# Rotary attention in a decoder kernel: another order of the steps around the softmax, and the keys' addition on another engine

## The reference

```python
def _L1_attn_ref(x, W_qkv, W_o1, W_o2, gamma):      # called with _layernorm(x), its result is added to x
    qkv = x @ W_qkv
    q, k, v = jnp.split(qkv, 3, axis=-1)
    q, k, v = (to_heads(q), to_heads(k), to_heads(v))
    apply_rope = lambda t: t * cos + rotate_half(t) * sin
    q, k = (apply_rope(q), apply_rope(k))
    dots = jnp.einsum('bhid,bhjd->bhij', q, k) * scale
    dots = jnp.where(causal, neg, dots)
    attn = jax.nn.softmax(dots, axis=-1)
    out = jnp.einsum('bhij,bhjd->bhid', attn, v)
    out = out.transpose(0, 2, 1, 3).reshape(b, n, INNER)
    out = jax.nn.relu(out @ W_o1) @ W_o2
    mean = jnp.mean(out, axis=-1, keepdims=True)
    var = jnp.var(out, axis=-1, keepdims=True)
    ...
```

## Time and profile before

| | before |
|---|---|
| median of 3 runs | 1791.98 us (1784.16 to 1795.23) |
| the profiled execution | 1798.92 us, span 1797.1 us |
| TensorE busy, share of the span | 1206.6 us, 67% |
| VectorE | 1063.3 us, 59% |
| ScalarE | 626.0 us, 35% |
| GpSimd | 665.7 us, 37% |
| first and last start of the stage (first transpose L1707 to the next stage's first, L550) | 385.1 and 636.7 us |

### The profile page before, as it was taken

How to read it: one execution, slowest core, us unless ns; L and a number is a source line. 1 busy time by engine, 2 the same in 40 slices (tenths; PEclk the granted TensorE clock), 3 DMA queues, 4 the chain that set the end, 5 groups by cost and what they waited for, 6 DMA issues and landing times. The chain is left out here.

```text
span 1797.1 us, 35666 instructions
## 1 busy us (share of the span) xinstructions
PE 1206.6 (67%) x14040; PEld 918.3 (51%) x14040; DVE 1063.3 (59%) x2911; ACT 626.0 (35%) x1479; POOL 665.7 (37%) x729
## 2 busy tenths in 40 slices
PE   7882438827888679374667444199839857666888
PEld 5652437726766646362345343088715616253556
DVE  4879611156999758615776657234379854444773
ACT  2541113306666646023553111022124334333443
POOL 3337444423555445532223114623343331413320
PEclk9885569969999889585877655599978765656788
DMA  9900046440000094040000010345310000000000
GB/s 256 132 2 2 29 118 179 143 130 2 3 2 3 3 136 58 17 120 3 1 1 16 9 24 7 102 139 179 120 35 2 1 1 2 1 1 1 1 2 24
DMA packets 74059, 90.19 MB, mean 50 GB/s; under 512 B 5823, under 2 KB 61186, under 8 KB 73248
## 3 DMA queue, kind: packets, MB, share of 16 engines
q1 hardware_dynamic: 67872, 77.94, 18.6%
q0 software_dynamic: 6016, 9.93, 1.6%
HBM read 57.60 MB, written 32.69 MB: 50 GB/s over the span
## 5 line engine op out<-in xcount | busy, mean ns | idle before, releaser
L846 POOL TENSOR_TENSOR arena<-arena,small 128x1024 f32<-128x1024 f32 x96 | 184.4, 1926 | 154.4 <-ACT arena L704 90.7
L394 POOL TENSOR_SCALAR var_eps<-moments 128x1 f32<-128x1 f32 (+1 forms) x136 | 33.6, 247 | 405.9 <-DVE moments L387 405.9
L606 PE MATMUL ps<-arena,q 64*64 64x512 f32 x768 | 129.9, 751 | 57.8 <-issue 20.6
L755 ACT ACTIVATE arena<-arena 128x1024 f32<-128x1024 f32 x92 | 97.3, 1058 | 179.1 <-DVE arena L920 127.9
L616 PEld LDWEIGHTS ps<-small,arena 128*128 128x128 f32 x736 | 101.8, 167 | 82.6 <-ACT arena L755 48.0
L616 PE MATMUL ps<-small,arena 128*128 128x128 f32 x736 | 124.0, 323 | 24.3 <-ACT arena L755 22.7
L628 PE MATMUL ps<-vx,arena 128*64 128x18 f32 x3072 | 126.6, 228 | 3.7 <-issue 3.0
L628 PEld LDWEIGHTS ps<-vx,arena 128*64 128x64 f32 x3072 | 116.5, 160 | 24.3 <-issue 20.4
L795 ACT COPY arena<-ps 128x512 f32<-128x512 f32 x192 | 104.6, 586 | 53.3 <-PE ps L616 52.3
L1857 POOL TENSOR_TENSOR arena<-arena 128x512 f32<-128x512 f32 x64 | 79.8, 1282 | 104.2 <-DVE arena L1875 104.2
L396 POOL TENSOR_TENSOR rstd<-var_eps,minus_half 128x1 f32<-128x1 f32 (+1 forms) x136 | 105.3, 774 | 11.3
(11 more groups left out here) (324 smaller groups left out, 2786.0 us busy)
## 6 DMA issues: line engine op xcount, KB each, us to landing
expert_ring<-L2f_in SPq DMA_DIRECT2D x23, 704.0 KB, 4.2
expert_ring<-L0f_in SPq DMA_DIRECT2D x23, 578.0 KB
slots_L0f<-blank SPq DMA_DIRECT2D x1, 8385.0 KB, 56.9
slots_L2f<-blank SPq DMA_DIRECT2D x1, 8385.0 KB, 56.8
small<-small_in SPq DMA_DIRECT2D x1, 4231.5 KB, 19.2
expert_ring<-L1f_in SPq DMA_DIRECT2D x8, 512.0 KB
arena<-slots_L0f SPq DMA_DIRECT2D x23, 129.0 KB, 3.1
arena<-slots_L2f SPq DMA_DIRECT2D x23, 129.0 KB, 3.6
```

The lines of the kernel that those rows point to most:

```text
L606: last = pe.matmul(c.ps[part(b), m], c.q[part(m), at:at + S], kx(t)[part(m), b * 512:(b + 1) * 512], start=True, stop=True)
L755: act.activation(buf(k), buf(k), ACT.Relu if sparse else ACT.Exp, scale=exp_scale).then_inc(s.probs_ready, 1)
L846: g.tensor_tensor(kx(t).rearrange("p (b h k) -> p b h k", b=2, k=S), bcast(of_tile, 2, HEADS // 2), bcast(bcast(c.w("head_of_row"), 2, S), ...
```

## The change

VectorE adds the products of the keys (`add_turned_keys`), GpSimd keeps those of the queries. In VectorE's step the measuring of `att` and the normalising now stand behind the maxima and ahead of the products, and they work on tiles one step older (k-4 and k-2). TensorE's `project_values` moves to the end of the step and works on the next tile; weighing and both output projections work on tile t-3, and the weighing stands ahead of the turning. ScalarE's exponentials are split 10, 2 and 4, with the copies of the weighed values (k-3) in front of those of the turned probabilities. A fourth place for values is the buffer `q`, which this sub-layer did not use. The three instructions of the residual become two `scalar_tensor_tensor`. GpSimd's second inversion works on tile k-4 in place of k-5.

```diff
-    values = lambda t: c.room(4 + t % 3)
+    value_places = [c.room(4), c.room(5), c.room(6), c.q[:]]
+    values = lambda t: value_places[t % 4]
...
-            for t in range(NT + 2):
+            for t in range(NT + 3):
                 if t < NT:
-                    project_values(t)
                     project(t, 0)
                     project(t, 1)
-                if t >= 2:
+                if t == 0:
+                    project_values(0)
+                if t >= 3:
+                    weigh_values(t - 3)
+                if 0 <= t - 2 < NT:
                     turn_probs(t - 2)
-                    weigh_values(t - 2)
-                    project_out(t - 2)
+                if t >= 3:
+                    project_out(t - 3)
                 if t < NT:
                     scores(t)
-                if t >= 2:
-                    project_mid(t - 2)
+                if t >= 3:
+                    project_mid(t - 3)
+                if t + 1 < NT:
+                    project_values(t + 1)
...
+            def take_values(t):
+                act.wait_ge(s.v_ps, t + 1)
+                if t >= 4:
+                    act.wait_ge(s.o_ps, t - 3)
+                act.copy(values(t), c.ps[:, 4:6].rearrange("p b n -> p (b n)")).then_inc(s.v_ready, 1)
...
+            for k in range(NT + 4):
+                if 0 <= k - 4 < NT:
+                    take_mid(k - 4)
+                if k < NT:
+                    take_values(k)
+                if 0 <= k - 1 < NT:
+                    soften(k - 1, range(10))
+                if 0 <= k - 3 < NT:
+                    take_weighed(k - 3)
+                if 0 <= k - 1 < NT:
+                    soften(k - 1, range(10, 12))
+                if 0 <= k - 2 < NT:
+                    take_turned_probs(k - 2)
+                if 0 <= k - 1 < NT:
+                    soften(k - 1, range(12, 16))
+                if 0 <= k - 3 < NT:
+                    rectify(k - 3)
...
                 if k < NT:
-                    for i, signal in enumerate((s.q_rotated, s.k_rotated)):
-                        g.wait_ge(s.by_sin, 2 * k + i + 1)
-                        for half in range(2):
-                            own_half = rotated[i][:, half * 512:(half + 1) * 512]
-                            g.tensor_tensor(own_half, own_half, sines[i][:, (1 - half) * 512:(2 - half) * 512], ALU.add)\
-                                .then_inc(signal, 1)
-                if 0 <= k - 5 < NT:
-                    invert(c, g, following, k - 5)
+                    g.wait_ge(s.by_sin, 2 * k + 1)
+                    for half in range(2):
+                        own_half = rotated[0][:, half * 512:(half + 1) * 512]
+                        g.tensor_tensor(own_half, own_half, sines[0][:, (1 - half) * 512:(2 - half) * 512], ALU.add)\
+                            .then_inc(s.q_rotated, 1)
+                if 0 <= k - 4 < NT:
+                    invert(c, g, following, k - 4)
...
+            def add_turned_keys(t):
+
+                v.wait_ge(s.by_cos, 2 * t + 2)
+                v.wait_ge(s.by_sin, 2 * t + 2)
+                for half in range(2):
+                    own_half = rotated[1][:, half * 512:(half + 1) * 512]
+                    v.tensor_tensor(own_half, own_half, sines[1][:, (1 - half) * 512:(2 - half) * 512], ALU.add)\
+                        .then_inc(s.k_rotated, 1)
...
             for k in range(NT + 6):
-                softened = 0 <= k - 1 < NT
-                if softened:
+                if 0 <= k - 1 < NT:
                     mask(k - 1)
                     find_max(k - 1)
+                if 0 <= k - 4 < NT:
+                    v.wait_ge(s.y_ready, k - 3)
+                    measure(v, own, c.att, k - 4)
+                if 0 <= k - 2 < NT:
+                    normalise(k - 2)
                 if k < NT:
                     rotate(k, 0)
                     rotate(k, 1)
+                    add_turned_keys(k)
                 t = k - 4
                 if 0 <= t < NT:
-                    scale(v, own, c.att, c.hn, t)
-                    v.wait_ge(own.normed, t + 1)
-                    v.tensor_tensor(c.hn[:, t], c.hn[:, t], c.w("L1_gamma"), ALU.mult).then_inc(s.weighted, 1)
+                    v.wait_ge(own.rstd, t + 1)
+                    v.scalar_tensor_tensor(out=c.hn[:, t], in0=c.att[:, t], scalar=own.moments_of[:, t, 0:1],
+                                           in1=c.w("L1_gamma"), op0=ALU.subtract, op1=ALU.mult).then_inc(s.weighted, 1)
                     v.wait_ge(s.weighted, t + 1)
-                    v.tensor_tensor(c.x[:, t], c.x[:, t], c.hn[:, t], ALU.add).then_inc(s.added, 1)
+                    v.scalar_tensor_tensor(out=c.x[:, t], in0=c.hn[:, t], scalar=own.rstd_of[:, t:t + 1],
+                                           in1=c.x[:, t], op0=ALU.mult, op1=ALU.add).then_inc(s.added, 1)
                     v.wait_ge(s.added, t + 1)
                     measure(v, following, c.x, t)
                 if 0 <= k - 5 < NT:
                     scale(v, following, c.x, c.h, k - 5)
-                if 0 <= k - 3 < NT:
-                    v.wait_ge(s.y_ready, k - 2)
-                    measure(v, own, c.att, k - 3)
-                if softened:
-                    normalise(k - 1)
```

More of the change, by code:

```diff
@@ L1689, in rotary_attention @@
     scores_ps = c.ps[:, 0:4, 0:256].rearrange("p r (m k) -> p r m k", k=S)
-    exps_of = lambda t: 2 + 3 * t if t < NT else 0
     head_of = lambda block, u: 8 * (block % 2) + 4 * u + block // 2
@@ L1800, in soften @@
             def soften(t, groups):
+                act.wait_ge(s.bias_ready, t + 1)
                 for g in groups:
@@ L1805, in soften, with take_mid, take_weighed, take_turned_probs @@
                                           accum_out=c.row_max[:, t, g:g + 1])
[L1806 to L1811, removed]
-                if 0 <= k - 3 < NT:
[L1813 to L1828, removed]
+                if groups[-1] == HEADS - 1:
+                    last.then_inc(s.exp_ready, 1)
+            def take_mid(t):
+                act.wait_ge(s.y_ps, t + 1)
+                act.copy(c.att[:, t], c.ps[:, 7, 0:P]).then_inc(s.y_ready, 1)
+            def take_values(t):
[3 more added lines that the diff above has]
+                act.copy(values(t), c.ps[:, 4:6].rearrange("p b n -> p (b n)")).then_inc(s.v_ready, 1)
+            def take_weighed(t):
+                act.wait_ge(s.o_ps, t + 1)
+                if t > 0:
+                    act.wait_ge(s.mid_ps, t)
+                for b in range(2):
+                    act.copy(outT[:, b * 512:(b + 1) * 512], c.ps[:, 6 + b]).then_inc(s.o_ready, 1)
+            def take_turned_probs(t):
                 for j in range(2):
@@ L1833, in _, with rectify @@
                     act.copy(probsT[:, j * 512:(j + 1) * 512], c.ps[:, 4 + j]).then_inc(s.probsT_ready, 1)
[L1834 to L1842, removed]
+            def rectify(t):
                 act.wait_ge(s.mid_ps, t + 1)
                 act.activation(c.oT[:, tok(t)], c.ps[:, 6, 0:P], ACT.Relu).then_inc(s.mid_ready, 1)
+            for q in range(QUARTERS):
+                act.wait_ge(s.turned_ps, q + 1)
+                act.copy(c.hT[:, quarter(q)], c.ps[:, q]).then_inc(s.turned, 1)
+            for k in range(NT + 4):
[15 more added lines that the diff above has]
+                    rectify(k - 3)
         @block.gpsimd
@@ L1894, in normalise @@
                 shaped = by_position(probs(t))
-                v.wait_ge(s.exp_ready, exps_of(t))
+                v.wait_ge(s.exp_ready, t + 1)
                 v.reciprocal(c.row_inv[:, t], c.row_max[:, t]).then_inc(s.inv_ready, 1)
```

## The result

The changed kernel takes 1802.64 us (median of 19 runs, 1792.7 to 1816.1), the kernel before 1793.12 in the same comparison: ratio 1.0068, 95% interval 1.0045 to 1.009. It is slower by 0.7%, and 1768 was forecast. The spans of the profiled executions lie 7.1 us apart (1804.2 after, 1797.1 before). Of these 4.5 are the rotary stage, 256.1 us (378.18 to 634.24) in place of 251.6; the parts ahead of it and behind it, whose instructions are unchanged, differ between the profiled executions of this document by up to 12 us (ahead) and 14 us (behind). The medians lie 9.5 apart; what the stage costs is taken from the traces.

What follows compares the result with a forecast made beforehand. The prediction took VectorE, or the chain through it, to bound the rotary stage. Fill 7.5 plus steady part 17.9 less drain 1.4 gave 24 us, from the median of 1791.98 to 1768, range 1758 to 1781.

Steps and rivals of the forecast that it cites:

- the cover on TensorE: TensorE's work within a step fits under the new pace: queries' half at +5.8 against VectorE's 6.06, covered by 0.3 us.
- the sum's steady part: Rotary tiles 3 to 15: 12 steps of 12.2 us, 146.5 in place of 164.5, summed as a gain of 17.9.
- The clock rival: TensorE's clock falls in the rotary stage's steady part: a step near 19 us, four eat the gain; 3 in 100.
- GpSimd's last 5.01 lie bare on the path: Of 7.69 us from first product to scores, GpSimd's four additions fill the last 5.01 and hold up the scores.
- 1.52 a step: Gain from VectorE adding the keys' products: scores start 6.17 us after the first product instead of 7.69.
- +12.2: TensorE's path through projections, weighing and ScalarE's copies lets the next scores start 12.2 us after the last scores' start.
- off the path: Three-instruction residual's 1.2 us each in the shadow of GpSimd's additions: said not to set the step, counted as nothing.
- its three pieces: Rotary step: scores to mask 1.64 us, mask to first product 4.42, first product to scores 6.17.
- no starving: Rival: VectorE's key additions each meet a GpSimd addition and cost 1.69 us, 2.0 a step more, 1800; 4 in 100.
- The ScalarE loop: Rival: output projection waits for ScalarE's copies; if 0.9 us late, a step is 12.7, total 1774; 12 in 100.
- The fill: Start of the rotary stage up to tile 3's scores: 7.5 us gained, up to 4 more if TensorE's clock stays high.
- The drain: From the last scores to the next stage's first transpose: one more round, 30.3 us instead of 28.9, loss 1.4.

Runs made afterwards that it cites:

- the half-page kernel: Changed kernel with 32 small matmuls (128 TensorE instructions) ahead of the rotary stage and 32 behind it: 1772.41 us, 0.9897 of the kernel before.
- the whole page: Changed kernel with 64 small matmuls (256 TensorE instructions) ahead of the rotary stage and none behind: 1.0047 of the kernel before.
- the kernel before moved: Kernel before with 23 small matmuls ahead of the rotary stage and 41 behind, so its scores fall on one instruction page: 1831.23 us, ratio 1.0219.

## Why the prediction was wrong

**The step that failed** is the cover on TensorE: "values 1.85 behind the scores' start", taken with "the scores, which take 1.59" and "The mask starts at 1.64 behind the scores' start (1.59 and a signal)". These durations hold only as long as TensorE has its instructions, and the sum put the wait for them at nothing. The change takes 164 instructions out of TensorE's stream ahead of tile 3's scores (one weighing, one output projection, one last projection, all now a step later), which puts the scores onto one packet; the kernel before has the same number a step, but its packets end inside the scores' first third and ahead of the turning. Its rotary stage shows no stop, and the prediction never counted instructions. The sign was there in another stage, where the same wait stands at 54 us, with a packet that landed at 52.42:

```profile
50.50 0.93 PE L628 MATMUL ps<-vx,arena 128*64 128x18 f32 x25
54.02 0.50 PE L628 MATMUL ps<-vx,arena 128*64 128x18 f32 x7 [2.58 <-issue]
```

The runs put a number on it: 172.8 us for the twelve steps with stops, 147.3 without, so 25.6 us were lost. The eight stops are 14.8 of that; of the other 10.8, by subtraction, 9.7 stand in the five steps in which TensorE's clock fell behind the stop. With that, the sum's steady part, forecast as a gain of 17.9, became a loss of 8.3.

**The clock rival** named the right engine and the wrong cause. I argued that there would be "no gap as long as the 5.8"; in or right behind a stop of 1.7 to 2.1 inside the scores the granted clock fell in five of eight cases. It carried 3 in 100.

**A reading that was wrong and did no harm.** The prediction says of the 7.69 from first product to scores that "GpSimd's last 5.01 lie bare on the path". Two paths ended together there: GpSimd's additions at 552.35 and TensorE's output projection, behind ScalarE's copies, at 552.66 (550.61 and 2.05), and the scores at 552.59 show no wait. With the keys' additions alone the 7.69 stays. Of a step of 13.80 they take 0.56 in the old order, the new order alone takes 0.14, and both together 1.53, so the "1.52 a step" wasn't a gain "of this part". The sum came out right because the cover counted the second path too, to "+12.2". The residual's waits for GpSimd did not lie "off the path" either: in the run with the keys' additions alone they are gone, and the mask comes 0.93 sooner although VectorE has those additions as well.

**What held**, measured where the stops are absent. The step: 12.27 against 12.2, each of its three pieces within 0.07. The twelve steps gave 17.2 (164.5 to 147.3) against 17.9. GpSimd's interference with the key additions was as described: 1.37 for both, no starving, and the two fused instructions cost 0.7 under the scores. VectorE was the bound: in the step shown it waits 0.34 for the scores and for nothing else. The ScalarE loop did not become it in the full change, and did in the kernel with the keys alone.

**Sizes that were off.** The fill gave 5.4 in place of 7.5 (the scores of tile 3 come 52.8 behind the stage's first transpose, 58.2 before): I had let TensorE's clock rise after the second tile as before, but the steps to tiles 2 and 3 took 13.71 and 13.26 in place of the 12.9 and 11.8 behind my sum, and the granted clock was down once more at 421.0. That the clock is the cause isn't shown. The drain lost 2.4 in place of 1.4 (31.4 from the last scores to the next stage, 28.95 before): two of its output projections ran at the lower clock level, 3.53 and 3.68, in place of one. In the changed kernel itself they did not, and its drain is 29.5. So the stage gains 20.2 where the stops are absent and I summed 24, and the half-page kernel's 1772 lies inside the range that was given for the change. The change as it stands does not.

**Open**: why the packet starts 2 to 3 us sooner in four of the changed kernel's steps, which have the same placing and no stop (their scores wait 0.6 us for VectorE in three of them, but so do others with a stop), and why the clock falls behind some stops only.

## What to carry to other kernels

Before a loop is made faster, count the instructions of its densest engine. Here 256 of them, done in 1.6 us, met a next page that came 3.3 to 3.7 us behind its beginning, and whether a page falls that way depends on everything ahead of it in the stream, not on the loop alone. When a change is slower for no wait in the program and the trace shows "issue" in the middle of a row of matmuls, look at when its instruction packets land. Then move the code by some 32 instructions with a filler, and by 256 as a control, before judging the change, and compare two orders only where neither has such a stop.

## What the runs showed of the hardware

- A stop of 1.7 to 2.4 us in TensorE's stream where 256 instructions pass in 1.6 us and packets of 16.4 KB bring them; gone when 32 instructions that take 2 us stand in the same packet, there in the last two tiles with 16.
- TensorE goes on 1.2 to 1.6 us after the packet has landed, at every such stop; the packet takes 0.9 to 1.4 us, and after a stop inside the scores the next one starts 1.0 to 1.5 us behind TensorE's going on (up to 2.4 in the last tile).
- The same stop put into the kernel before costs it 2.2%, with no other edit.
- TensorE's granted clock fell from its 2.4 GHz level in or right behind five of the changed kernel's eight stops of 1.7 to 2.1 us (0.76 as the mean over the 7.1 us that follow one), seven of eleven with the whole page, eleven of twelve in the kernel before moved; the values' projection, 3.58 in place of 1.88, shows it.
- VectorE's additions of two SBUF tensors right behind a GpSimd addition: 1.37 for two of 512 elements, 0.77 and 0.68, so that the first lost about 0.1.
